# One graph layer on one Trainium2 core: the bias adds of GpSimd moved behind the edge loop, edges prepared in four groups, a one-hot copied, weight loads on two queues

## The reference

```
xn = _layernorm(x, axis=-1)
h = spmm(xn); z0 = spmm(h); A0 = softmax(z0 @ W0.T + b0)        # graph part, 4 equal heads
z1 = spmm(A0); A1 = softmax(z1 @ W1.T + b1); gnn = tanh(concat(A0, A1) + h)
q, k, v = xn @ wq.T, xn @ wk.T, xn @ wv.T                       # attention part, linear
mix = (q @ (LN(k).T @ LN(v)) / S) @ wo.T + bo
x = x + gnn + mix
x = x + ffn(_layernorm(x))                                      # 8 experts, one for each token
```

## Time and profile before

| what | value |
|---|---|
| median of 3 runs | 1226.55 us (1225.81 to 1226.73) |
| the profiled execution | 1236.39 us, span 1234.6 us |
| PE busy | 1126.5 us (91%) |
| DVE busy | 722.2 us (58%) |
| ACT busy | 309.1 us (25%) |
| POOL busy | 165.3 us (13%) |
| granted clock, mean | 0.952 |

### The profile page before, as it was taken

The page is one execution under the profiler, slowest core; times in us unless marked ns, Lnnn a source line. Parts: engine busy times, 40 slices in busy tenths (PEclk is TensorE's granted clock), DMA queues, the critical chain, the costliest instruction groups (busy, mean ns, idle before and its releaser), DMA issues.

```text
span 1234.6 us, 14147 instructions
## 1 busy us (share of the span) xinstructions
PE 1126.5 (91%) x4909; PEld 713.7 (58%) x4909; DVE 722.2 (58%) x1650; ACT 309.1 (25%) x1012; POOL 165.3 (13%) x203
## 2 busy tenths in 40 slices
PE   4688988979999999999997999999999479999995
PEld 2355655556666666666674444545558446666664
DVE  7999999978776777777760011114546404444333
ACT  3446555511221212112220111102111122222220
POOL 1123434410000000000000000000233411111111
PEclk8789888989999999999998999999999679999998
DMA  6101110121333333342227988787984363333410
GB/s 166 13 7 44 44 43 1 44 85 44 130 120 135 136 121 120 120 163 85 86 85 290 351 323 301 269 307 265 307 297 156 138 204 108 113 121 118 159 60 7
DMA packets 65862, 175.40 MB, mean 142 GB/s; under 512 B 16607, under 2 KB 49146, under 8 KB 53758
## 3 DMA queue, kind: packets, MB, share of 16 engines
q1 hardware_dynamic: 53230, 123.12, 29.2%
q10 hardware_dynamic: 8240, 43.30, 8.8%
q0 software_dynamic: 4320, 8.04, 1.8%
HBM read 113.82 MB, written 63.01 MB: 143 GB/s over the span
## 4 chain that ended last, share of the span: by engine, by line
PE 75%; DVE 15%; issue 4%; ACT 2%; another core or an unknown queue 2%; ACTq 1%; DMA 1%; POOL 0%; POOLq 0%; DVEq 0%
PE ps L1411 19%; PE ps L1558 18%; PE ps L1394 10%; PE ps L1664 9%; PE ps L1653 9%; PE ps L1317 2%; PE ps L1436 2%; DVE W L938 2%; DVE RY L935 1%; PE ps L1378 1%; PE ps L1364 1%; PE ps L1413 1%; DVE RING L983 1%; DVE RING L977 1%
## 5 line engine op out<-in xcount | busy, mean ns | idle before, releaser
L1411 PE MATMUL ps<-RING,XX 128*128 128x512 f32 x600 | 285.2, 598 | 4.9 <-DVE W L993 4.7
L1558 PE MATMUL ps<-RING,RY 128*128 128x512 f32 (+2 forms) x750 | 280.8, 533 | 6.7 <-issue 6.7
L1558 PEld LDWEIGHTS ps<-RING,RY 128*128 128x128 f32 x750 | 137.2, 197 | 133.2 <-issue 131.1
L1394 PEld LDWEIGHTS ps<-RING 128*128 128x128 f32 x1250 | 167.7, 197 | 46.1 <-issue 44.8
L1394 PE MATMUL ps<-RING 128*128 128x128 f32 x1250 | 175.0, 282 | 2.2 <-DVE RING L986 2.2
L692 ACT COPY RING<-ps 128x512 f32<-128x512 f32 (+1 forms) x157 | 91.7, 584 | 335.1 <-PE ps L1394 318.4
L1411 PEld LDWEIGHTS ps<-RING,XX 128*128 128x128 f32 x600 | 104.1, 193 | 78.3 <-issue 78.1
L977 DVE TENSOR_TENSOR RING<-iota_n,RY 128x512 f32<-128x512 f32 (+1 forms) x157 | 108.0, 688 | 67.4 <-PE ps L1394 63.3
L595 POOL DMA_INDIRECT xbuf_dram<-XX,sidx x25 | 25.4, 1017 | 643.2 <-DVE sidx L1240 637.7
L983 DVE TENSOR_TENSOR RING<-iota_n,RY 128x512 f32<-128x512 f32 (+1 forms) x157 | 108.9, 694 | 0.0
L986 DVE TENSOR_TENSOR RING<-RING,RY 128x512 f32<-128x512 f32 x132 | 89.8, 680 | 0.0
(11 more groups left out here) (246 smaller groups left out, 1264.1 us busy)
## 6 DMA issues: line engine op xcount, KB each, us to landing
RING<-adj_dram SPq DMA_DIRECT2D x62, 1280.0 KB
adj_dram<-RING ACTq DMA_DIRECT2D x31, 1280.0 KB, 4.5
XT<-in_L_ffn_w SPq DMA_DIRECT2D x8, 1024.0 KB, 7.9
RING<-in_L_ffn_w SPq DMA_DIRECT2D x8, 1024.0 KB, 6.7
rbuf_dram<-W SPq DMA_DIRECT2D x8, 516.0 KB, 5.3
RING<-rbuf_dram SPq DMA_DIRECT2D x8, 516.0 KB, 3.8
xbuf_dram<-W SPq DMA_DIRECT2D x8, 512.0 KB, 3.3
RING<-xbuf_dram SPq DMA_DIRECT2D x8, 512.0 KB, 4.8
```

The lines of the kernel that those rows point to most:

```text
L1394: last = nc.tensor.matmul(o[:, i * P:(i + 1) * P], h[:, 0, i, :], h[:, 1, i, :], start=True, stop=(j != s))
L1411: last = nc.tensor.matmul(ps[:, ACC + dd, :], w, at, start=(j == 0), stop=True, skip_group_check=True)
L1558: last = nc.tensor.matmul(o, (Y if l == 0 else S0)[:, j, :], RING[:, slot_of[g % 5], i * across + first:i * across + first + w], start=(j ...
```

## The change

Four things, in the code of the first 280 us:

1. GpSimd's bias adds leave the edge loop and come behind it, 25 in a row, behind waits for the weights and for all `bn_stats`.
2. `GROUPS` has four groups instead of six: tiles 0-1, 2-5, 6-15 and 16-24. Two helper arrays are bf16 instead of f32, and `quo` lies in `W`. The statistics are still taken in four parts, but their variances and scales in two (`LG`): tiles 0-6 and 7-24. The `bn_stats` of parts 1 to 3 come at `it` 0, 1 and 2 (before: 0, 2, 4), and `prepare(0)` comes between the first variance and its scales.
3. `ohp` is a copy of `ohs` with another order of elements instead of a second comparison; `iota_sp`, which only that needed, is gone.
4. Five of ACT's sixteen weight transfers are issued by SP, after the windows of group 0; the transfers of `x` follow at once. ACT makes one square root whose result nobody reads, ahead of the wait for its first product.

```diff
-GROUPS = ((0, 2), (2, 6), (6, 11), (11, 16), (16, 21), (21, 25))
+GROUPS = ((0, 2), (2, 6), (6, 16), (16, 25))
-XG = ((0, 6), (6, 13), (13, 19), (19, 25))
-STATS_AT = {0: 1, 2: 2, 4: 3}
+XG = ((0, 7), (7, 13), (13, 19), (19, 25))
+LG = ((0, 7), (7, 25))
...
-                for x in {0: (1,), 1: (2, 3)}.get(g, ()):
+                if g == 0:
+                    for to, src in ((wo_n, half("L0_mix_wo")), (wq_n, half("L0_mix_wq")), (W0_n, a["L0_gnn_W0"]),
+                                    (W1_n, a["L0_gnn_W1"]), (b1_n, a["L0_ffn_b1"])):
+                        sp.dma_start(to, src).then_inc(s_w, 16)
+                for x in {0: (1, 2, 3)}.get(g, ()):
...
-            gp.wait_ge(s_w, 16 * NWL)
             for it in range(NT + KV_LAG + 1):
...
-                if it < NT:
-                    gp.wait_ge(s_xn, it + 1)
-                    gp.wait_ge(s_stats, it + 1)
-                    gp.tensor_tensor(X1[:, it, :], X1[:, it, :], bo_b[:, :], ALU.add).then_inc(s_bo, 1)
...
+            gp.wait_ge(s_w, 16 * NWL)
+            gp.wait_ge(s_stats, NT)
+            for j in range(NT):
+                gp.wait_ge(s_xn, j + 1)
+                gp.tensor_tensor(X1[:, j, :], X1[:, j, :], bo_b[:, :], ALU.add).then_inc(s_bo, 1)
...
+            act.wait_ge(s_const, 2)
+            nc.scalar.activation(rsum[:, 0, 0:1], ones_f[:, 0:1], ACT.Sqrt)
...
-                v.tensor_tensor(ohp[b].rearrange("p (c s i) -> p c s i", s=NR, i=2),
-                                iota_sp.rearrange("p (s i) -> p s i", i=2).unsqueeze(1).to_broadcast([P, C2, NR, 2]),
-                                g.rearrange("p (c i) -> p c i", i=2).unsqueeze(2).to_broadcast([P, C2, NR, 2]), ALU.is_equal)
+                v.tensor_copy(ohp[b].rearrange("p (c s i) -> p s c i", s=NR, i=2), ohs[b].rearrange("p (s c i) -> p s c i", c=C2, i=2))
...
             stats(0)
+            variances(0)
+            prepare(0)
             scales(0)
-            prepare(0)
             spread(0)
...
-                if it - 1 in STATS_AT:
-                    scales(STATS_AT[it - 1])
-                if it in STATS_AT:
-                    stats(STATS_AT[it])
+                if it == 3:
+                    scales(1)
+                if it < 3:
+                    stats(it + 1)
+                if it == 2:
+                    variances(1)
```

More of the change, by code:

```diff
@@ L143, in graph_program @@
         val_w = hb[:, 900:1350]
-        srcf, dstf, quo, diag, inv = (hb[:, 1350 + 90 * i:1440 + 90 * i] for i in range(5))
+        srcf, dstf = hb[:, 1350:1530], hb[:, 1530:1710]
+        inv, diag = hb[:, 1710:1800].bitcast(BF16), hb[:, 5274:5364].bitcast(BF16)
         grp = hb[:, 1800:2025].bitcast(BF16)
@@ L149, in graph_program @@
         fresh = hb[:, 3609:3843].bitcast(BF16)
-        iota_sp = hb[:, 3844:3870].bitcast(BF16)
         ohs = [hb[:, 3870 + 234 * i:4104 + 234 * i].bitcast(BF16) for i in range(2)]
+        ohp = [hb[:, 4806 + 234 * i:5040 + 234 * i].bitcast(BF16) for i in range(2)]
         scan = [hb[:, 4338 + 234 * i:4572 + 234 * i].bitcast(BF16) for i in range(2)]
-        ohp = [hb[:, 4806 + 234 * i:5040 + 234 * i].bitcast(BF16) for i in range(2)]
         wq_n = hb[:, 5376:5888].rearrange("p (r n) -> p r n", r=2)
@@ L165, in graph_program @@
         sq = W[:, 3372:3884]
+        quo = W[:, 3884:4064]
         dflat = W[0:EP, 0:425].bitcast(I32)
@@ L342, in graph_program @@
         s_khat = sem("s_khat")
+        s_hscale = sem("s_hscale")
         s_kvt = sem("s_kvt")
@@ L416, in _ @@
             flat = lambda name: a[name].rearrange("(p t) -> p t", t=ET)
+            half = lambda name: a[name].rearrange("(r p) n -> p r n", p=P)
             sp.dma_start(dflat, flat("dst")).then_inc(s_dst, 16)
@@ L542, in _ @@
             gp.iota(ints[:, 900:900 + SW], pattern=[[0, NR], [1, WC]], base=0, channel_multiplier=0).then_inc(s_const, 1)
-            gp.iota(ints[:, 1400:1400 + 2 * NR], pattern=[[1, NR], [0, 2]], base=0, channel_multiplier=0).then_inc(s_const, 1)
             gp.wait_ge(s_const, 2)
@@ L550, in _ @@
                              base=0, pattern=[[1, P]], channel_multiplier=-1).then_inc(s_const, 1)
-            gp.wait_ge(s_const, 10)
+            gp.wait_ge(s_const, 9)
             gp.memset(blk, 0.0).then_inc(s_blk, 1)
@@ L628, in _ @@
             act.dma_start(X1[:, 0:XG[0][1], :], a["x"][0:XG[0][1] * P, :].rearrange("(j p) d -> p j d", p=P)).then_inc(s_x[0], 16)
-            for to, src in ((wo_n, half("L0_mix_wo")), (wq_n, half("L0_mix_wq")),
-                            (W0_n, a["L0_gnn_W0"]), (W1_n, a["L0_gnn_W1"]), (b1_n, a["L0_ffn_b1"]), (gate_w[:, :, :], half("L0_ffn_gate_w")),
-                            (bo_b[:, :], a["L0_mix_bo"].partition_broadcast(P)), (gb1_b[:, :], a["L0_gnn_b1"].partition_broadcast(P)),
+            for to, src in ((gate_w[:, :, :], half("L0_ffn_gate_w")), (bo_b[:, :], a["L0_mix_bo"].partition_broadcast(P)), (gb1_b[:, :], a["L0_gnn_b1"].partition_broadcast(P)),
                             (gate_b[:, :], a["L0_ffn_gate_b"].partition_broadcast(P)),
@@ L650, in roots @@
             def roots(g):
-                t = slice(*XG[g])
+                t = slice(*LG[g])
                 act.wait_ge(s_var, g + 1)
@@ L655, in normal @@
             def normal(j):
-                act.wait_ge(s_rstd, [j < t1 for _, t1 in XG].index(True) + 1)
+                act.wait_ge(s_rstd, 1 if j < LG[0][1] else 2)
                 nc.scalar.activation(XN[:, j, :], X1[:, j, :], ACT.Identity, bias=lnb[:, j:j + 1], scale=lnr[:, j:j + 1]).then_inc(s_xn, 1)
@@ L720, in _ @@
                     squares(it)
-                if it in STATS_AT:
-                    roots(STATS_AT[it])
+                if it == 2:
+                    roots(1)
                 if 1 <= it <= NT:
@@ L856, in _ @@
             v.tensor_scalar(fresh, ints[:, 900:900 + SW], 1.0, None, ALU.min)
-            dve.wait_ge(s_const, 10)
+            dve.wait_ge(s_const, 9)
             dve.wait_ge(s_blk, 3)
@@ L867, in _ @@
             v.tensor_scalar(base_i[:, :], base_f, 0.0, float(E - WIN), ALU.max, ALU.min).then_inc(s_base, 1)
-            v.tensor_copy(iota_sp, ints[:, 1400:1400 + 2 * NR])
             v.tensor_copy(before[:, :], before_f)
@@ L953, in head_scale @@
                 link(v.tensor_scalar(r, r, 0.5, None, ALU.mult))
-                link(v.reciprocal(r, r))
+                v.reciprocal(r, r).then_inc(s_hscale, 1)
+                dve.wait_ge(s_hscale, g + 1)
             def normed(m):
@@ L1028, in kv_tail, with stats, variances @@
                 v.engine_nop().then_inc(s_kvp, 1)
-            def stats(g):
-                dve.wait_ge(s_x[g], 16 if XG[g][1] < NT else 32)
-                for j in range(*XG[g]):
+            def stats(x):
+                dve.wait_ge(s_x[x], 16 if XG[x][1] < NT else 32)
+                for j in range(*XG[x]):
                     v.bn_stats(bst[:, j, :], X1[:, j, :]).then_inc(s_stats, 1)
-                dve.wait_ge(s_stats, XG[g][1])
-                variance(slice(*XG[g]))
+            def variances(g):
+                dve.wait_ge(s_stats, LG[g][1])
+                variance(slice(*LG[g]))
             def scales(g):
-                t = slice(*XG[g])
+                t = slice(*LG[g])
                 rstd(t, g + 1)
@@ L1317, in flip @@
                 return nc.tensor.transpose(dst, src, ident[0:n, 0:n])
-            pe.wait_ge(s_const, 10)
+            pe.wait_ge(s_const, 9)
             pe.wait_ge(s_cnt0, 1)
```

## The result

| | before | after |
|---|---|---|
| median | 1226.21 us (1225.81 to 1226.73, 4 runs) | 1211.17 us (1208.44 to 1212.95, 4 runs) |
| the profiled execution | 1236.39 us, span 1234.6 | 1211.29 us, span 1209.5 |
| PE busy | 1126.5 us (91%) | 1112.9 us (92%) |
| DVE busy | 722.2 us (58%) | 708.3 us (59%) |
| granted clock, mean | 0.952 | 0.967 |

The ratio of the medians is 0.9875 (95% interval 0.9856 to 0.9894): the changed kernel is 15 us faster. The forecast was 7.8 us faster. The time lies in the range, but the gain is twice the one that was worked out, so the question is which terms of the sum are wrong. One run of all that stand behind this document, 1359.54 us at a granted clock of 0.828 with the comparison back, is far slower than the five others of its kernel and is left out of that kernel's median and ratio.

What follows compares the result with a forecast made beforehand. Before 280 us DVE and TensorE were taken as both near the limit in each five-tile block. Edge stage -15.1 and adds behind it +7.3 give -7.8: 1228.6, less 9.8 for the profiled execution's excess, 1218.7 us; range 1209 to 1225.

Steps and rivals of the forecast that it cites:

- The start: Up to the first edge blocks: 4.5 us gained, 3.2 from statistics, waits and transfers and 1.3 from the adds taken away.
- The groups: Edge loop: two `prepare` fewer gain 5.3 and 4.9 us, the two longer ones cost 1.5 and 1.2.
- The statistics: Two variances and two scales fewer: 2.6 and 1.2 us gained in the start, 1.2 in the block behind it.
- the adds' share in the loop: Bias adds leaving the edge loop: gains of 1.3, 0.9, 0.5 and 0.5 us, from some seven that met DVE.
- the second price: Rest of a five-tile block, from the big operand's end to `head_var`: 23.8 us, called DVE's pace, against TensorE's 24.85.
- the copy at no gain: Second one-hot in the edge loop: copy taken at 0.39 us like the comparison; ends -5.5 and +6.1 us over 25.
- the cost behind the loop: Adds behind the edge loop: 9 x 0.49 = 4.4 us up to L993, six more in `kv_tail` 2.9, together +7.3.
- B: Rival: behind the loop the adds are hidden, so 15.1 us gained and 1211.4 us; chance 0.20.
- C: Rival: the copy goes one element at a time, 0.245 us more per tile, +4.6, 1223.3 us; chance 0.13.
- E: Rival: slower, the copy runs at the scan's 1.133 us, giving 1236 us; chance 0.04.
- F: Rival: the shorter `prepare` list gains nothing, TensorE being the limit; 1223.8 us if half counts; chance 0.04.
- D: Rival: the start gains nothing, windows or `x` coming later still behind the weights; 1223.2 us; chance 0.09.

Runs made afterwards that it cites:

- the comparison back: The changed kernel with the comparison for the second one-hot instead of the copy, and its constant: median 1214.25 us, ratio 0.9906 to the kernel before.
- the adds alone: The kernel before with only the 25 bias adds moved behind GpSimd's loop: median 1226.36 us, ratio 1.0000 to the kernel before.
- the other parts: The changed kernel with the bias adds back in GpSimd's loop, all else changed: median 1211.02 us, ratio 0.9869 to the kernel before.
- the adds paced: The changed kernel with the adds behind the attention matrix wait, each waiting for a read in `mixed`: median 1203.94 us, ratio 0.9818 to the kernel before.
- after again: The changed kernel unchanged, one more profiled execution: 1213.45 us.
- no root ahead: The changed kernel without ACT's square root that nobody reads: median 1210.67 us, ratio 0.9883 to the kernel before.

## Why the prediction came out as it did

**Right.** What bounds each part, and where the stalls would stand. The start: 3.3 to 4.6 us at tile 4 against 4.5, with DVE's waits of 1.5 and 1.7 us forecast as 1.5 and 1.3. The groups: 6.1 of 7.5 us. The statistics: 3.5 to 4.5 of 5.0. The mechanism behind the loop: GpSimd slips an add between each two of DVE's operations, they stretch to 1.14 to 1.22 us (forecast 1.17), and TensorE waits 8.57 us for the first strip (forecast 9).

**Wrong: the adds' share in the loop.** The step was "Of the 25, some seven met DVE in a part that counts", 3.2 us together, 2.7 of them ahead of tile 24, with the others beside "DVE's scan and reduce". The runs show 4.1 us for the adds alone and 6.4 among the other parts. I counted what an add does to the DVE operation beside it, and took the operation behind it on GpSimd as fixed. It was that one, L575, which the add pushed from the reduction onto L935 and L938: a stretch of 0.48 us, in L938 at 11 of the 25 tiles. In the kernel alone a part of this was hidden, since TensorE was near its limit (the 4.3 us of waits in `head_var`); with DVE's first part shorter, it counted. For the same reason the second price, DVE's 23.8 us for the rest of a block, was not DVE's own pace: three stretched L938 were in it. Nor was the 4.3 us of a `prepare`, which had 1 us of GpSimd in it: some of what I gave to the groups belongs to the adds. Without the stretches DVE needs 6.7 us for a tile, TensorE 6.87, and the block falls to TensorE's 36.3 when its clock holds.

**Wrong: the copy at no gain.** I compared 0.39 with 0.393 us, durations. What DVE's next operation sees is the start-to-start time, 0.30 and 0.20 us: 2.5 to 3.0 us over 25 tiles, and 3.0 at tile 24 with the comparison back. The end of the range for the copy (a gain of 5.5 us) held it. These two sizes, 3.7 and 3.0 us too small, are over the 2.7 us that are missing at tile 24, with the groups and the statistics each short by about 1 in the other direction; the parts don't add up exactly, since TensorE takes over as the limit.

**Too dear: the cost behind the loop.** Forecast 7.3 us, 6.8 with the half microsecond gained behind 235.32. The way from tile 24 to the matrix grew from 56.55 to 60.59 us in the profiled execution, 4.0, and to 62.3 in two others, 5.8. The 9 x 0.49 = 4.4 before L998 measured 3.9 (29.27 us from `head_var` to TensorE's restart against 25.39 with the adds paced), the six in `kv_tail` 1.9 of 2.9 (9.35 us from L1020 to the next comparison against 7.4): six of its small operations were hit, but by 0.10 to 0.48 us. The sum had no term for TensorE's clock, which differs between these executions and hides or adds up to 2 us.

**The rivals.** B gave 1211.4 us, the measured time, but by luck and not by its mechanism: the adds were not hidden. C and E, a slow copy, and F, TensorE as a limit that swallows the shorter `prepare`, did not come; D neither. In F's reason there is truth: TensorE is the limit, but at 36.3 us a block, not at 43.

**What stays open.** At the matrix the three executions with the adds behind the loop and the weights on SP (after, after again, no root ahead) lie 10.6 to 14.7 us ahead of before, 12.8 in the mean, and the medians 15.0. The other 2 us would lie behind, where the code is the same. There the three took 930.6 to 932.4 us and the kernel before 932.4 and 942.7, so single executions scatter by as much; no run was made for them. The shorter types of two helper arrays were not run alone; a `prepare` of 90 columns took 3.14 us with them and 3.22 without. The change also has a wait of DVE behind the last operation of `head_scale` (`s_hscale`) that its description leaves out; the next operation starts 0.44 us behind that one, 0.43 before. That TensorE's clock holds behind one stall and falls behind an equal one was seen, not explained.

## What to carry to other kernels

When work is taken from GpSimd, whose operations stretch DVE's, follow the instruction behind it as well: its new place decides which DVE operation stretches. Work that nobody waits for should be spread by a wait on a slow consumer, one at a time; 25 adds in a row cost behind the loop all that they had cost in it, and paced they cost nothing that a run shows. For DVE, take the cost of a short operation from start to start of a row and the next, not from its duration.

## What the runs showed of the hardware

A 128x256 f32 add on GpSimd and the DVE operations on SBUF in these rows shut each other out in turns: the add waits for the end of the DVE operation (L575: 1.83 us instead of 0.64 to 0.68) and the next DVE operation starts its work 0.48 to 0.5 us late (1.85 for 1.37, 1.17 for 0.68), while the reduction that reads PSUM, 0.64 us with an add beside it in the rows of before, is not stretched. The Trainium skill, "GPSIMD Engine Reference" (1, Specifications), says that GpSimd's SBUF interfaces are shared with VectorE, with contention against instructions in a two-port mode or with two SBUF inputs; the trace agrees, and has the price that the page does not give. GpSimd's own short additions (128x26) waited too: 1.13 us instead of 0.24 beside DVE's scan of two SBUF inputs.
